# A mixture-of-experts stage with the token chunk as its outer loop and gates read back from DRAM

## The chip, the core and the metric

The kernel runs on one core of a Trainium2 chip. The metric is the device time of the whole program in microseconds. Engines are named as in the profile: PE (TensorE matmul) and PEld (its weight load), DVE (VectorE), ACT (ScalarE), POOL (GpSimd) and SP (SyncE, which here only issues DMAs).

## What is computed

A Mamba-2 block and a mixture-of-experts (MoE) block, each with a layernorm before and after and a residual, on 8 x 256 tokens of 256 channels. The change is in the second block:

```python
router = xf @ gate_w.T                                   # 8 experts
probs = softmax(router); top_p, top_i = top_k(probs, 2)
combine = zeros((n, 8)).at[arange(n)[:, None], top_i].set(top_p)
h = silu(xf @ expert_fc1[e].T) * (xf @ expert_fc2[e].T)  # 176 hidden rows an expert
y = einsum('ne,enc->nc', combine, h @ expert_proj[e].T)  # all 8 experts, then weighted
shared = (silu(xf @ shared_fc1.T) * (xf @ shared_fc2.T)) @ shared_proj.T   # 704 hidden rows
y = y + sigmoid(xf @ shared_gate_w.T) * shared
x = x + layernorm(y)
```

## The kernel before

The first three quarters of the time are the Mamba block, which the change leaves alone but for two tuples of PSUM bank numbers (L196, L197). The MoE block begins at L1205.

**Tiles.** The hidden rows of all eight experts (8 x 176 = 1408, exactly 11 tiles of 128) and of the shared expert (704, five and a half tiles) are laid end to end and padded to FT = 17 tiles. The 2048 tokens are CHUNKS = 4 chunks of UT = 512 columns. One *step* j is one tile f with one chunk c, and there are 68 of them. Every float32 product is made of three passes in the format float32r, high x high, high x low and low x high, so that each weight and activation is first split in two parts: ACT copies the high part, and POOL or DVE subtracts it from the whole to get the low one.

**One step.** PE's `hidden(j)` (L1320) makes fc1 into PSUM bank 4 or 5 and fc2 into bank 6 or 7, six matmuls each. `route_weight` (L1355) makes in bank 0 or 1, by one bf16 matmul of a one-hot matrix `f_hot` with the gates `combT`, the gate of each hidden row. ACT's `silu` (L1479) writes `sl`; DVE's `gated` (L1582) multiplies it by fc2 to `hm`, and `routed` (L1588) by the gate to `hc`. ACT's `high` (L1488) and POOL's `low` (L1734) split `hc` into `h_hi` and `h_lo`. PE's `project` (L1359) makes six matmuls of it into banks 2 and 3, and DVE's `add_up` (L1592) adds these to `outT` in SBUF. PE emits `hidden(j)`, the gate matmul and `project(j - 2)` in this order.

**Order.** The tile is the outer loop: after a head of AHEAD = 3 tiles, taken chunk by chunk before the gates are known (`early`, L1338), tiles 3 to 16 run in a hardware loop (`pair_loop`, L1261), with four chunks each; each tile's weights are loaded (`reload`, L1284) and split (ACT L1461, POOL L1731) as they come up. All four chunks end with the last tile, so the last layernorm (turning the sum back to rows by PE transposes, L1391; statistics, L1696; scaling and residual; the four output DMAs, L1300) stands behind the last step, for all four.

**The way in.** Before the first step the kernel ends the Mamba block's residual and makes the MoE input: `stats`/`scales`/`residual` on DVE (L221 to L251), `stats2`/`scales2` (L1557), the square roots `row_std`, `row_std2` and the scaling `normed` (L1467) on ACT, `turn_normed` (L1305) on PE, `high_x` (L1474) on ACT and `low_x` (L1573) on DVE. Each engine's order is written out by hand.

Of the kernel before, what the change touches and what calls it, by code (L numbers as in the profile page):

```python
# [5 lines left out]
def mamba_moe_sandwich_kernel(nc, x_d, wx_d, wz_d, wo_d, par_d, wdt_d, dtb_d, alog_d,  # L6
# [17 lines left out]
    KH = HID // 128  # L24
# [25 lines left out]
    with outer:  # L50
# [145 lines left out]
        BANK1 = (2, 0, 4, 2)  # L196
        BANKV = (5, 5, 5, 7)  # L197
# [1005 lines left out]


        sb = make_sb(outer)  # L1205
        AHEAD = 3
        END = CHUNKS * FT
        EARLY = CHUNKS * AHEAD
        PSTEPS = [(c, f) for c in range(CHUNKS) for f in range(AHEAD)]
        BUF = (2, 3, 0)  # L1210
        xo = sb("xo", [128, TILES, HID], fp32)
        wf_raw = sb("wf_raw", [128, 2, 768], fp32)
        wf_hi = sb("wf_hi", [128, AHEAD + 1, 768], f32r)
        wf_lo = sb("wf_lo", [128, AHEAD + 1, 768], f32r)
        combT = sb("combT", [CROWS, TOK], bf16)
        f_hot = sb("f_hot", [CROWS, FT * 128], bf16)
# [5 lines left out]
        ident_b = sb("ident_b", [128, 128], bf16)  # L1222
        lgT = sb("lgT", [NLG, TOK], fp32)
# [4 lines left out]
        gts = shared[:, TILES * HID:TILES * (HID + E * E)].rearrange("p (t e o) -> p t e o", t=TILES, e=E)  # L1228
        eqs = sb("eqs", [128, TILES, E, E], fp32)
        rank = sb("rank", [128, TILES, E], fp32)  # L1230
        comb = sb("comb", [128, TILES, ROUTES], fp32)
        comb_r = sb("comb_r", [128, TILES, ROUTES], fp32)
        cparts = sb("cparts", [128, TILES, PARTS, ROUTES], bf16)
        sl = sb("sl", [128, 2, UT], fp32)
        hm = sb("hm", [128, EARLY, UT], fp32)

        hot_raw = hm[0:CROWS, 7:EARLY, :].rearrange("p s t -> p (s t)")[:, 0:FT * 128]
        hc = sb("hc", [128, 2, UT], fp32)
        h_hi = sb("h_hi", [128, CHUNKS, UT], f32r)
        h_lo = sb("h_lo", [128, CHUNKS, UT], f32r)  # L1240
# [6 lines left out]
        s_q, s_e, s_cp = sem("s2_shifted_logits"), sem("s2_exp"), sem("s2_route_parts")  # L1247
        s_ct, s_cc = sem("s2_combT"), sem("s2_combT_copied")
        f1_done, f2_done, g_done, p_done = sem("fc1_done"), sem("fc2_done"), sem("route_weight_done"), sem("moe_proj_done")
        sl_done, hhi_done, wfh_done = sem("fc1_silu_done"), sem("h_hi_done"), sem("moe_w_hi_done")  # L1250
        hm_done, hc_done, fa_done = sem("h_done"), sem("h_scaled"), sem("moe_proj_added")
# [5 lines left out]
        BANK2 = (6, 0, 2, 0)  # L1257
        LBANK = (2, 3, 0, 1)
        BANK4 = (4, 6, 0, 2)

        def pair_loop(eng, body):  # L1261


            body(AHEAD, 1, 1, BUF[AHEAD - 1], False)
            body(AHEAD + 1, 2, 0, 1, False)
            with eng.Fori(1, (FT - AHEAD) // 2 - 1) as i:
                body(2 * i + AHEAD, i + 1, 1, 0, False)
                body(2 * i + AHEAD + 1, i + 2, 0, 1, False)
            body(FT - 2, FT // 2 - 1, 1, 0, True)
            body(FT - 1, FT // 2, 0, 1, True)  # L1270

        SUMB = (2, 6, 4, 2)
        ADDS = CHUNKS - EARLY

        with nc.Block() as block:
            @block.sync
            def _(sp):
                for f in range(2):
                    sp.dma_start(wf_raw[:, f, :], wf_d[f, :, :]).then_inc(s_f[f], 16)
                for dst, src in ((wg_raw[:, :, :], wg_d.rearrange("p (k n) -> p k n", k=KH)),  # L1280
                                 (tie[:, :], tie_d), (hot_raw, f_hot_d)):
                    sp.dma_start(dst, src).then_inc(s_in, 16)

                def reload(f, par):  # L1284
                    sp.wait_ge(wfl_done, f + 1)
                    sp.dma_start(wf_raw[:, par, :], wf_d[f + 2, :, :]).then_inc(s_f[par], 16)

                for f in range(AHEAD):
                    reload(f, f % 2)

                def body(f, filled, par, before, last):
                    if not last:
                        reload(f, par)
                pair_loop(sp, body)
                for i in range(CHUNKS):
                    if i < CHUNKS - 1:
                        sp.wait_ge(s_o4, i + 1)
                    else:
                        sp.wait_ge(s_sc4, TILES)
                    sp.dma_start(out_v[:, quarter(i), :], xo[:, quarter(i), :]).then_inc(s_out, 16)  # L1300
                sp.wait_ge(s_out, 16 * CHUNKS)

            @block.tensor
            def _(pe):
                def turn_normed(i):  # L1305
                    pe.wait_ge(s_n, QT * i + QT)

                    if i == 0:
                        pe.wait_ge(s_rn, 2)
                    elif i == 3:  # L1310
                        pe.wait_ge(s_l2, KH * 2)
                    else:
                        pe.wait_ge(s_x1, QT * (2 if i == 1 else 4))
# [6 lines left out]
                def hidden(j, par, c):  # L1320
                    need(pe, hm_done, j - 1)
                    if isinstance(j, int) and j == 0:
                        pe.wait_ge(s_x1, QT * 3)
                    for which in range(2):
                        n = 0
                        for whl, xhl in ((wf_hi, xnT_hi), (wf_hi, xnT_lo), (wf_lo, xnT_hi)):
                            for k in range(KH):
                                w0 = 256 * k + 128 * which
                                mm = pe.matmul(PS[:, 4 + 2 * which + j_parity(j, c), :], whl[:, par, w0:w0 + 128],  # L1329
# [3 lines left out]
                        mm.then_inc(f2_done if which else f1_done, 1)  # L1333

                def j_parity(j, c):
                    return j % 2 if isinstance(j, int) else c % 2

                def early(p):  # L1338
                    c, f = PSTEPS[p]
                    pe.wait_ge(wfl_done, f + 1)  # L1340
                    pe.wait_ge(s_l2, KH * c + KH)
                    hidden(p, BUF[f], c)

                def logits(i):
                    pe.wait_ge(s_gl, 1)
                    pe.wait_ge(s_l2, KH * 3 if i < 2 else KH * CHUNKS)
# [8 lines left out]
                def route_weight(f, c, bank):  # L1355
                    hot = f_hot[:, 128 * f:128 * f + 128] if isinstance(f, int) else f_hot[:, bass.ds(128 * f, 128)]
                    pe.matmul(PS[:, bank, :], hot, combT[:, UT * c:UT * c + UT], start=True, stop=True).then_inc(g_done, 1)  # L1357

                def project(j, par, c):  # L1359
                    pe.wait_ge(hlo_done, j + 1)  # L1360
                    need(pe, fa_done, j + ADDS)
                    shares(2, par, c, True, True)

                def shares(bank, par, slot, first, last):
                    for m in range(KH):
                        w0 = 512 + 128 * m
# [464 lines left out]
```

## Time and profile before

| | us |
|---|---|
| the three runs | 1510.77, 7722.83, 7724.07 (median 7722.83) |
| the profiled execution, from first to last instruction | 1511.5 |
| of it PE busy | 1416.6 (94%) |
| DVE, ACT, POOL busy | 1192.8, 989.4, 868.5 |
| Mamba block, until its last matmul | to 1138.4 |
| MoE block, its first instruction to the end | 1141.2 to 1511.5 |

Two of the three runs are some 6212 us longer than the third, with which the profiled execution agrees; the profile shows nothing of such a wait. Instructions overlap on PE, so that the duration of a matmul (0.39 us) is about twice the distance between two starts; the distance is what counts. The granted TensorE clock is given as a share of 2.4 GHz: 1.00 is 2.4 GHz and 0.50 is 1.2 GHz.

### The profile page before, as it was taken

To read this page: it belongs to the slowest core of one execution; us is meant where nothing else is said; L and a number is where in the kernel's file an instruction comes from. 1 tells how busy PE (TensorE), PEld (TensorE's weight loads), DVE (VectorE), ACT (ScalarE), POOL (GpSimd) and SP (SyncE) were. 2 spreads that over 40 slices of the span, in tenths; PEclk is the share of its full clock that TensorE was granted. 3 is DMA by queue.
4 is the path that set the end of the run, shared out by engine and by line. 5 is a ranking of instruction groups with operands and counts; after the bars stand their busy time and mean duration, and the time that the engine had idled before them with its cause. 6 is when DMAs were issued, how large, how long until landed. Compare 5 with 4: busy or idle time off the path is not lost. (4 is left out here: it accounts for less than half of the span.)

```text
span 1511.5 us, 25812 instructions
## 1 busy us (share of the span) xinstructions
PE 1416.6 (94%) x7484; PEld 1013.6 (67%) x7484; DVE 1192.8 (79%) x1749; ACT 989.4 (65%) x1450; POOL 868.5 (57%) x758
## 2 busy tenths in 40 slices
PE   4699999999999999999999999999987999999995
PEld 3466667767676776767667677766765667777774
DVE  6799888988997988999898899989757555555556
ACT  4587877878787787877778787877746322333333
POOL 3256676767676666767676676777562143333333
PEclk9799999999999999999999999999988999999998
DMA  4100000010000000000000000000011000000001
GB/s 115 43 13 25 19 18 25 5 33 3 24 18 18 24 3 27 9 24 18 18 25 3 18 18 24 17 18 4 4 57 60 11 11 22 21 21 21 21 0 56
DMA packets 26219, 34.47 MB, mean 23 GB/s; under 512 B 10420, under 2 KB 20276, under 8 KB 26090
## 3 DMA queue, kind: packets, MB, share of 16 engines
q1 hardware_dynamic: 26116, 33.42, 7.3%
q14 instruction: 77, 0.62, 0.1%
q8 instruction: 26, 0.43, 0.1%
HBM read 30.13 MB, written 3.28 MB: 22 GB/s over the span
## 5 line engine op out<-in xcount | busy, mean ns | idle before, releaser
L346 DVE SCALAR_TENSOR_TENSOR acc<-PS,par_a,acc 128x510 f32<-128x510 f32 (+2 forms) x576 | 422.1, 738 | 25.6 <-ACT acc L310 20.0
L1126 POOL TENSOR_TENSOR g_lo<-gy,g_hi 128x512 fp32r<-128x512 f32 x128 | 171.4, 1339 | 215.8 <-ACT g_hi L862 215.7
L1135 POOL TENSOR_TENSOR ssq<-ssq,y 128x256 f32<-128x256 f32 x256 | 262.6, 1026 | 13.2
L1120 POOL TENSOR_TENSOR gy<-y,sz 128x512 f32<-128x512 f32 x128 | 193.4, 1511 | 89.8 <-DVE y L998 57.8
L1736 POOL TENSOR_TENSOR h_lo<-hc,h_hi 128x512 fp32r<-128x512 f32 x68 | 87.6, 1290 | 205.0 <-ACT h_hi L1491 204.9
L985 DVE SCALAR_TENSOR_TENSOR shared<-shared,cbm 128x1024 f32<-128x1024 f32 x96 | 141.4, 1473 | 67.7 <-ACT shared L849 67.6
L310 ACT ACTIVATE acc<-PS,par_a 128x512 f32<-128x512 f32 x192 | 149.3, 777 | 31.2 <-PE PS L293 27.7
L985 DVE SCALAR_TENSOR_TENSOR M<-M,cbm 128x1024 f32<-128x1024 f32 x96 | 150.7, 1569 | 4.9 <-ACT M L849 1.4
L293 PE MATMUL PS<-xnT_hi,wx_hi 128*128 128x512 f32 x384 | 143.3, 454 | 6.5 <-DVE acc L346 5.8
L849 ACT ACTIVATE M<-PS 128x1024 f32<-128x1024 f32 x96 | 98.5, 1026 | 66.8 <-PE PS L687 66.5
L1491 ACT ACTIVATE h_hi<-hc 128x512 fp32r<-128x512 f32 x68 | 43.0, 632 | 151.1 <-DVE hc L1590 151.1
L844 ACT ACTIVATE sz<-PS 128x512 f32<-128x512 f32 x128 | 76.4, 598 | 92.9 <-PE PS L293 89.7
L1582 DVE TENSOR_TENSOR hm<-PS,sl 128x512 f32<-128x512 f32 x68 | 47.0, 691 | 110.0 <-PE PS L1329 100.1
L687 PE MATMUL PS<-R,L 91*128 91x512 bf16 x384 | 117.3, 387 | 16.2 <-ACT shared L849 13.3
L293 PE MATMUL PS<-xnT_hi,wx_lo 128*128 128x512 f32 x384 | 122.5, 401 | 0.0
L730 PE MATMUL PS<-g_hi,wo_hi 128*128 128x512 f32 x256 | 109.1, 426 | 13.6 <-DVE outT L1014 8.0
L293 PE MATMUL PS<-xnT_lo,wx_hi 128*128 128x512 f32 x384 | 121.8, 399 | 0.0
L849 ACT ACTIVATE shared<-PS 128x1024 f32<-128x1024 f32 x96 | 98.3, 1024 | 12.7 <-PE PS L687 12.3
L730 PE MATMUL PS<-g_hi,wo_lo 128*128 128x512 f32 x256 | 103.2, 403 | 0.0
L730 PE MATMUL PS<-g_lo,wo_hi 128*128 128x512 f32 x256 | 102.6, 401 | 0.0
L713 PE MATMUL PS<-M,xdt 128*64 128x256 f32 (+1 forms) x1024 | 97.3, 332 | 0.5 <-issue 0.5
L713 PE MATMUL PS<-shared,xdt 128*64 128x256 f32 (+1 forms) x1024 | 97.3, 332 | 0.1
(198 smaller groups left out, 3194.6 us busy)
## 6 DMA issues: line engine op xcount, KB each, us to landing
wf_raw<-in_wf SPq DMA_DIRECT2D x17, 384.0 KB, 3.1
wraw<-in_wx SPq DMA_DIRECT2D x8, 768.0 KB, 4.5
wraw<-in_wz SPq DMA_DIRECT2D x8, 512.0 KB, 3.4
R<-cs_parts SPq DMA_DIRECT2D x256, 3.0 KB
wraw<-in_wo SPq DMA_DIRECT2D x8, 512.0 KB, 3.4
L<-cs_parts SPq DMA_DIRECT2D x64, 36.0 KB
outT<-in_x SPq DMA_DIRECT2D x4, 512.0 KB, 6.0
shared<-in_x SPq DMA_DIRECT2D x4, 512.0 KB, 3.9
```

The lines of the kernel that those rows point to most:

```text
L293: mm = pe.matmul(PS[:, bank, :], lhs[:, k, c0:c0 + 128], rhs[:, k, UT * q:UT * q + UT], start=(n == 0), stop=(n == 3 * KH - 1))
L310: act.activation(acc[:, k % 3, :], PS[:, XBANK[k], :], ACT.Identity, scale=par_a[:, TAPS * k + TAPS - 1:TAPS * k + TAPS], bias=par_a[:, TA ...
L346: dve.scalar_tensor_tensor(dst[:, :, s:SEQ], src[:, :, 0:SEQ - s], par_a[:, TAPS * k + TAPS - 1 - s:TAPS * k + TAPS - s], dst[:, :, s:SEQ] ...
L687: mm = pe.matmul(PS[:, 2 + s, :], L[:, b, s, 128 * blk:128 * blk + 128], R[:, b, min(blk, 1), s, :, :], start=True, stop=True)
L713: mm = pe.matmul(o, lhs, rhs, start=(c == 0), stop=(c == 1))
L730: mm = pe.matmul(PS[:, bank, :], lhs[:, ct, 128 * m:128 * m + 128], rhs[:, ct, :], start=(ct == 0 and n == 0), stop=(ct == CT - 1 and n == 2))
L849: act.activation(M[par][:, BORDER[n], :, :].rearrange("p h (s i) -> p s h i", s=2), PD.rearrange("p s (h i) -> p s h i", i=64), ACT.Exp).t ...
L985: dve.scalar_tensor_tensor(M[par][:, blk, :, :], M[par][:, blk, :, :], 1.0, cbm[:, 128 * blk:128 * blk + 128].unsqueeze(1).to_broadcast([1 ...
L1120: pool.tensor_tensor(gy[:, half, :, :], y[:, half, :, :], sz[:, 2 * half:2 * half + 2, SEQ * b:SEQ * b + SEQ], ALU.mult).then_inc(gy_done, 1)
L1126: pool.tensor_tensor(g_lo[:, cts, ts], gy[:, half, :, :], g_hi[:, cts, ts].bitcast(fp32), ALU.subtract).then_inc(lo_done, 1)
L1135: pool.tensor_tensor(tok, tok, y2[:, half, cc, :], ALU.add).then_inc(ssq_link, 1)
L1736: pool.tensor_tensor(h_lo[:, c, :], hc[:, c % 2, :], h_hi[:, c, :].bitcast(fp32), ALU.subtract).then_inc(hlo_done, 1)
```

## The change

The stage is rewritten around the token chunk. The 17 tiles' weights stay in SBUF in 11 slots (`SLOTS`): the six shared tiles come first, for all four chunks (24 steps), then the eleven expert tiles for chunk 0, 1, 2, 3 (44 steps), while six of them refill the slots of shared tiles. No hardware loop is left. The projection is summed over a chunk's tiles in PSUM banks 2 and 3 (`ZB`) and read once. The half-filled tile 16 is made by 6 matmuls with fc1 and fc2 side by side, instead of 12. The shared sum is multiplied by its sigmoid afterwards (`gate_shared`); the experts' gates are written to DRAM once, read back with each expert's row repeated over its partitions (`load_gate`, 256 KB a step), and multiplied to the silu on POOL (`gate`). The last layernorm of chunk c runs in steps of chunk c + 1. What was `combT`, `f_hot` and the bf16 parts of the gates is gone.

The diff, cut to its core:

```diff
-        BANK1 = (2, 0, 4, 2)
-        BANKV = (5, 5, 5, 7)
+        BANK1 = (2, 0, 2, 0)
+        BANKV = (5, 5, 5, 5)
...
+        END_S, END_E = 6, 11
+        STEPS = [(c, f) for c in range(CHUNKS) for f in range(END_E, FT)] + \
+                [(c, f) for c in range(CHUNKS) for f in range(END_E)]
+        SLOTS = 11
+        GSLOTS = 4
+        HR = 3
+        NORM_AT = (3, 6, 8)
+        LOGITS_AT = (10, 11)
+        GATES_AT = 12
+        GATES_OUT = 21
+        REFILL = (21, 22, 23, 26, 28, 30)
...  SP
+                def load_tile(n):
+                    if n >= 2:
+                        sp.wait_ge(wfl_done, n - 1)
+                    sp.dma_start(wf_raw[:, n % 2, :], wf_d[TILE_AT[n], :, :]).then_inc(s_f[n % 2], 16)
+                def load_gate(n):
+                    c, f = STEPS[SHARED + n]
+                    if n >= GSLOTS:
+                        sp.wait_ge(sg_done, n - GSLOTS + 1)
+                    for e, p, q in segments(f):
+                        src = gate_rows[e:e + 1, UT * c:UT * c + UT]
+                        sp.dma_start(g_sb[p:q, n % GSLOTS, :], src.to_broadcast([q - p, UT])).then_inc(s_g[n % GSLOTS], 16)
+                sp.wait_ge(s_cc, 1)
+                sp.dma_start(gate_rows[0:E, :].rearrange("e (t p) -> (e t) p", p=128), gT[:, 0, :]).then_inc(s_gd, 16)
+                sp.dma_start(gate_rows[E, :].rearrange("(t p) -> t p", p=128), gT[0:TILES, 1, :]).then_inc(s_gd, 16)
+                sp.wait_ge(s_gd, 32)
+                for n in range(GSLOTS):
+                    load_gate(n)
+                load_shared_gate(0)
...  PE
-                    for which in range(2):
+                    for which in range(1 if f == HALF else 2):
...
-                def route_weight(f, c, bank):
-                    pe.matmul(PS[:, bank, :], hot, combT[:, UT * c:UT * c + UT], start=True, stop=True).then_inc(g_done, 1)
...
+                def project(j):
+                    c, f = STEPS[j]
+                    s, r = SLOT[f], rows_of(f)
+                    pe.wait_ge(hlo_done, j + 1)
+                    if first_of(j):
+                        need(pe, fa_done, c if j < SHARED else CHUNKS + c)
+                    for m in range(KH):
+                        for n, (whl, hhl) in enumerate(((wf_hi, h_hi), (wf_hi, h_lo), (wf_lo, h_hi))):
+                            mm = pe.matmul(PS[:, ZB + m, :], whl[0:r, s, w0:w0 + 128], hhl[0:r, j % HR, :],
+                                           start=(first_of(j) and n == 0), stop=(last_of(j) and n == 2))
+                for j in range(END):
+                    hidden(j)
+                    if j >= 2:
+                        project(j - 2)
+                    if j in NORM_AT:
+                        turn_normed(1 + NORM_AT.index(j))
+                    if j in LOGITS_AT: ...
+                    if j > SHARED + END_E and STEPS[j][1] == 3:
+                        turn_sum(STEPS[j][0] - 1)
+                project(END - 2)
+                project(END - 1)
+                turn_sum(CHUNKS - 1)
...  ACT
+                split(0)
+                row_std2(0)
+                norms(act, 1, TILES - QT, TILES)
+                normed(0)
+                row_std(act, 2)
+                split(1)
+                high_x(0)
+                row_std(act, 3)
+                split(2)
+                for j in range(END):
+                    silu(j)
+                    high(j)
+                    if j == 0: split(3); row_std2(1)
+                    if j == 1: split(4); normed(1); ...
+                    if j == 2: split(5)
+                    if j == 3: row_std2(2); row_std2(3)
+                    if j == NORM_AT[0]: high_x(1)
+                    if j == 5: normed(2)
+                    if j == NORM_AT[1]: high_x(2); normed(3)
...
+                    if j > SHARED + END_E and STEPS[j][1] == 3: row_std4(STEPS[j][0] - 1)
+                    if j > SHARED + END_E and STEPS[j][1] == 4: finish(STEPS[j][0] - 1)
...  DVE
-                    dve.tensor_tensor(hc[:, par, :], PS[:, par, :], hm[:, slot, :], ALU.mult).then_inc(hc_done, 1)
...
+                    if j > SHARED + END_E and STEPS[j][1] == 1: add_experts(STEPS[j][0] - 1)
+                    gated(j)
+                    if j == 0: scales(dve, 3); residual(dve, 3); stats2(1); scales2(1)
+                    if j == 1: stats2(2)
+                    if j == 2: stats2(3)
+                    if j == 4: scales2(2); scales2(3)
+                    if j == NORM_AT[0] + 1: low_x(1)
+                    if j in REFILL: split(SLOTS + REFILL.index(j))
+                    if j >= SHARED and STEPS[j][1] == 8: gate_shared(STEPS[j][0])
+                    if j > SHARED + END_E and STEPS[j][1] == 3: stats4(STEPS[j][0] - 1)
+                    if j > SHARED + END_E and STEPS[j][1] == 4: scales4(STEPS[j][0] - 1)
...  POOL
+                def gate(j):
+                    pool.wait_ge(s_g[n % GSLOTS], 16 * loads)
+                    pool.wait_ge(sl_done, j + 1)
+                    need(pool, hm_done, j - 1)
+                    pool.tensor_tensor(sg[:, j % 2, :], sl[:, j % 2, :], g_sb[:, n % GSLOTS, :], ALU.mult).then_inc(sg_done, 1)
+                for j in range(END):
+                    if j < 3: split(3 + j)
+                    if j >= SHARED: gate(j)
+                    if j > SHARED: low(j - 1)
+                    if j < SHARED: low(j)
+                    if 10 <= j < 10 + SLOTS - END_S: split(END_S + j - 10)
+                    if j > SHARED + END_E and 4 <= STEPS[j][1] < 4 + QT:
+                        pool.tensor_tensor(xo[:, n, :], xo[:, n, :], x1[:, n, :], ALU.add).then_inc(s_o4, 1)
```

(A condition and its calls are put on one line here, and waits that the text does not speak of are left out.)

## Rows read from the trace of the kernel before

**Rows 1.** Busy time by stretch of the MoE block (header, three stretches).
```profile
core 0: us, PE busy (x) PEld busy (x) DVE busy (x) ACT busy (x) POOL busy (x), PEclk, DMA share, GB/s
1150.00:1156.30 6.30, 6.30 (x21) 5.03 (x21) 5.30 (x26) 3.94 (x8) 1.37 (x2) 0.54 0.44 125
...
1223.70:1487.30 263.60, 263.60 (x1066) 189.48 (x1065) 143.69 (x167) 78.71 (x126) 95.56 (x69) 1.00 0.06 17
1487.30:1511.50 24.20, 7.10 (x45) 5.59 (x43) 18.76 (x51) 10.06 (x22) 8.30 (x4) 0.77 0.26 87
```

**Rows 2.** Timeline of one steady step, PE: start, duration, instruction, count.
```profile
1303.71 0.63 PE L1329 MATMUL PS<-xnT_hi,wf_hi 128*128 128x512 f32 x2
...
1306.05 0.63 PE L1329 MATMUL PS<-xnT_hi,wf_lo 128*128 128x512 f32 x2
1306.61 0.38 PE L1357 MATMUL PS<-combT,f_hot 27*128 27x512 bf16 x1
1306.92 0.50 PE L1368 MATMUL PS<-h_hi,wf_hi 128*128 128x512 f32 x1
1307.26 0.39 PE L1368 MATMUL PS<-h_lo,wf_hi 128*128 128x512 f32 x1
```

**Rows 3.** Timeline of the same steady stretch, the other engines.
```profile
1305.31 0.60 ACT L1482 ACTIVATE sl<-PS 128x512 f32<-128x512 f32 x1 [0.98 <-PE PS L1329]
1306.78 0.69 DVE L1582 TENSOR_TENSOR hm<-PS,sl 128x512 f32<-128x512 f32 x1 [1.65 <-PE PS L1329]
1308.31 0.63 ACT L1491 ACTIVATE h_hi<-hc 128x512 fp32r<-128x512 f32 x1 [2.40 <-DVE hc L1590]
1308.62 1.23 DVE L1595 TENSOR_TENSOR outT<-PS,outT 128x1024 f32<-128x1024 f32 x1 [0.42 <-PE PS L1368]
1309.02 1.29 POOL L1736 TENSOR_TENSOR h_lo<-hc,h_hi 128x512 fp32r<-128x512 f32 x1 [3.33 <-ACT h_hi L1491]
```

**Rows 4.** Timeline of the way into the MoE block.
```profile
1141.18 0.82 SPq L1279 DMA_DIRECT2D wf_raw<-in_wf  x2
1143.96 2.07 ACT L1471 ACTIVATE xo<-shared,acc 128x256 f32<-128x256 f32 x4 [0.29 <-DVE acc L1571]
1146.40 0.83 ACT L1461 ACTIVATE wf_hi<-wf_raw 128x768 fp32r<-128x768 f32 x1
1148.59 1.28 DVE L1576 TENSOR_TENSOR xnT_lo<-PS,xnT_hi 128x512 fp32r<-128x512 f32 x2
1149.78 1.39 DVE L1560 BATCH_NORM_STATS2 acc<-shared 128x6 f32<-128x256 f32 x4
1149.96 1.19 PE L1329 MATMUL PS<-xnT_hi,wf_hi 128*128 128x512 f32 x2 [2.78 <-DVE xnT_lo L1576]
1155.53 1.65 DVE L250 SCALAR_TENSOR_TENSOR shared<-PS,acc,shared 128x256 f32<-128x256 f32 x4
1155.76 1.28 ACT L1482 ACT_TABLE_LOAD   x1
1155.82 1.85 POOL L1731 TENSOR_TENSOR wf_lo<-wf_raw,wf_hi 128x768 fp32r<-128x768 f32 x1 [4.93 <-ACT wf_hi L1461]
```

**Rows 5.** DMA issues: tensors, queue, count, size, median us to landing.
```profile
wf_raw<-in_wf SPq DMA_DIRECT2D x17, 384.0 KB, 3.1
```

**Rows 6.** Timeline of the end: last projection, last turn, last scaling.
```profile
1493.11 0.40 PE L1368 MATMUL PS<-h_hi,wf_lo 128*128 128x512 f32 x1
...
1495.11 1.09 PE L1391 MATMUL PS<-ident,outT 128*128 128x128 f32 x8 [0.74 <-DVE outT L1595]
...
1506.50 1.70 ACT L1549 ACTIVATE xo<-xo,acc 128x256 f32<-128x256 f32 x4 [2.94 <-DVE xo L1724]
```

**Rows 7.** Timeline in the Mamba block: one POOL product twice, one DVE product.
```profile
460.62 1.30 POOL L1120 TENSOR_TENSOR gy<-y,sz 128x512 f32<-128x512 f32 x1 [1.33 <-ACT sz L844]
...
469.66 2.28 POOL L1120 TENSOR_TENSOR gy<-y,sz 128x512 f32<-128x512 f32 x1
...
468.92 1.87 DVE L985 SCALAR_TENSOR_TENSOR shared<-shared,cbm 128x1024 f32<-128x1024 f32 x1
```

More of the change, by code:

```diff
@@ L1288, in _ @@
[L1288 to L1300, printed above, removed]
@@ new lines, in _ @@
+                for n in range(END_S, SLOTS + 2):
+                    load_tile(n)
+                sp.wait_ge(s_cc, 1)
[5 more added lines that the diff above has]
+                load_shared_gate(0)
@@ L1525, in _ @@
-                for p in range(7, EARLY - 1):
-                    silu(p, p % 2)
-                for p in range(EARLY):
-                    high(p, p % CHUNKS)
-                    if p == 1:
-                        silu(EARLY - 1, (EARLY - 1) % 2)
-                def body(f, filled, par, before, last):
-                    for c in range(CHUNKS):
-                        j = CHUNKS * f + c
-                        silu(j, c % 2)
-                        high(j, c)
-                        if c == 2 and not (isinstance(f, int) and f == FT - 1):
-                            split(f + 1, filled + par, 1 - par, 1 - par)
@@ L1540, in _, with high, row_std4, finish @@
-                pair_loop(act, body)
-                for i in range(CHUNKS):
+                def high(j):
+                    r = rows_of(STEPS[j][1])
+                    act.wait_ge(hm_done, j + 1)
+                    need(act, p_done, j - HR + 1)
+                    act.activation(h_hi[0:r, j % HR, :], hm[0:r, j % 2, :], ACT.Copy).then_inc(hhi_done, 1)
+                def row_std4(i):
                     act.wait_ge(s_ag4, 2 * i + 2)
                     act.activation(std[0][:, quarter(i)], mv[0][:, quarter(i), 1], ACT.Sqrt, bias=epsc[:, 0:1]).then_inc(s_sd4, 1)
+                def finish(i):
@@ L1682, in body @@
-                def body(f, filled, par, before, last):
-                    for c in range(CHUNKS):
-                        j = CHUNKS * f + c
-                        gated(j, c % 2, c % 2)
-                        dve.wait_ge(hm_done, j + 1)
-                        routed(j, c % 2, c % 2)
-                        if not (isinstance(j, int) and j - 2 < EARLY):
-                            add_up(j - 2, (c - 2) % CHUNKS)
-                        elif PSTEPS[j - 2][1] == AHEAD - 1:
-                            first_sum(PSTEPS[j - 2][0])
@@ L1742, in _ @@
-                split(AHEAD, 1, 1)
-                for p in range(EARLY):
-                    low(p, p % CHUNKS)
-                def body(f, filled, par, before, last):
-                    for c in range(CHUNKS):
-                        low(CHUNKS * f + c, c)
-                        if c == 2 and not (isinstance(f, int) and f == FT - 1):
-                            split(f + 1, 1 - par, 1 - par)
-                pair_loop(pool, body)
-                for i in range(CHUNKS - 1):
-                    pool.wait_ge(s_sc4, QT * i + QT)
-                    pool.tensor_tensor(xo[:, quarter(i), :], xo[:, quarter(i), :], x1[:, quarter(i), :], ALU.add).then_inc(s_o4, 1)
+                for n in range(3):
+                    split(n)
```

644 lines of the change are left out of this document (343 added, 301 removed).

## Prediction

> **What bounds the kernel now.** I read the busy time by stretch first, for where PE is the bound, then the timeline of one steady step, for what PE's time there is made of, then the timelines of the way in and the end, where PE waits. From 1223.7 to 1487.3 PE is busy all the time at the full clock [rows 1]. These are the last 56 of the 68 steps, 263.6 / 56 = 4.707 us each; DVE, ACT and POOL are busy 143.7, 78.7 and 95.6 us of it. So PE's stream is the time, and what leaves it is gained in full as long as the new waits stay inside the slack. At both ends it is otherwise: the first step starts at 1149.96, after a wait of 2.78 us for the low part of the input [rows 4], and runs at a granted clock of 0.54, which is the 1.2 GHz level for most of the stretch [rows 1]; and of the last 24.2 us PE works 7.1.
>
> **PE's stream, term by term.** From 1303.71 to 1306.05 ten matmuls start, one every 0.234 us [rows 2]. Eighteen of them are 4.21 us. A step takes 4.71, so the gate matmul costs 0.50, although it is one of nineteen: it starts 0.33 us after the one before, the next comes 0.31 later and the one after that 0.34 [rows 2], so its neighbours lose time too. It goes from all 68 steps: 68 x 0.50 = 34 us. If what follows it (0.34 against 0.234) were a cost of beginning `project` and stayed, 27 us would go; where `project` ends and `hidden` begins, nothing of the kind is seen, so I take 34. The half tile saves 6 matmuls in 4 chunks, 24 x 0.234 = 5.6 us. Hidden and projection are then 816 - 24 + 408 = 1200 matmuls, logits 24 as before.
>
> I sum the new kernel from its own start, since the way in is reordered.
>
> **The way in.** ACT's queue now begins with `split(0)`, which waits for the weight tile. It is issued at 1141.18 [rows 4] and lands 3.1 us later [rows 5], 1144.3; the split takes 0.83 [rows 4]. Before, the square root and the scaling stood ahead of it, the scaling from 1143.96. So the scaling now runs from about 1145.8 to 1147.9. `row_std(2)` and `split(1)` stand before `high_x(0)`, but `low_x(0)` no longer waits behind `residual(2)` (1.65 us, [rows 4]). I get the first hidden at 1151.2, 1.2 us later than before. It runs at 1.2 GHz again: 12 matmuls cost about 5.1 us instead of 2.8, +2.3.
>
> Then the small work of the second layernorm, which was spread around eleven steps without projection, sits between steps that need the whole chain silu, `gated`, `high`, `low`. I walked the four queues with the durations of [rows 3, 4] (silu 0.60, gated 0.69, high 0.63, low 1.29, split 0.83 on ACT and 1.85 on POOL, scaling 2.07, statistics 1.39, residual 1.65, each change of ACT's table 1.28). ACT changes between square root and silu five times before step 5. PE's waits come out as: `hidden(2)` 0.4 us, for gated(0), behind split(2) and a table; `project(0)` 2.0, for low(0), since POOL has split(3) ahead of it and that waits for ACT; `hidden(3)` 1.1, for gated(1), since silu(1) waits for row_std2(1), which waits for residual and statistics on DVE; `project(1)` 1.9, for low(1), behind split(4); `hidden(6)` 2.2, for the low part of chunk 1, `low_x(1)`, behind the square roots and a table. Together 7.6 us. From `hidden(7)` on, at 1188.4, the queues have caught up.
>
> **Steady shared steps.** 4.21 us, half tile 2.81. DVE has gated and at most one of ranking, splitting, copying a sum (1.23 for 1024 columns, [rows 3]) in one step: hidden behind PE. Gates are transposed and copied in step 21; write, wait, read back is two DMA round trips. At 3.1 us each and six issues of some 0.4 they are back before silu(24), about 11 us later; and `gated(24)` is needed by `hidden(26)` only 7 us after that. Cost nothing; a round trip twice as long would still cost nothing.
>
> **Steady expert steps.** The chain of a step: silu 0.60, POOL's product `gate` (nearest row: POOL's product of two 128x512 tiles, 1.30, [rows 7]), gated 0.69, high 0.63, low 1.29. ACT can't start the next silu before its high, so the loop ACT, POOL, DVE, ACT takes 0.60 + 1.30 + 0.69 + 0.63 and four hand-overs, about 3.6 us against PE's 4.21. low(j) stands behind gate(j + 1) on POOL and ends 3.5 us after fc1 of step j + 1; `project(j)` comes 5.6 us after it. 2.1 us of slack, no cost. POOL is busy 2.6 of 4.2. Loads of 256 KB four steps ahead (17 us) have 3.1 us of landing to hide.
>
> The upper bound for `gate` is 2.28, the same product beside a DVE product of SBUF operands (1.87 [rows 7], where 1024 columns take 1.23 in [rows 3]). The Trainium skill states this ("SBUF — State Buffer", "Who interferes with whom"): a DVE instruction with two SBUF inputs and a GpSimd one that reads SBUF exclude each other. By that rule the moved work is exposed, as POOL now runs twice as often; the trace agrees in the Mamba block. Here `gated` has one input in PSUM, so only the six splits and four `gate_shared` on DVE meet POOL, 1.2 us at most each, inside the 2.1; by the rule as by the row the sum is unchanged.
>
> **Chunk boundaries, three of them.** In step f = 3 PE turns the sum, DVE takes statistics, ACT the square root with two table changes (2.56); in step f = 4 `finish` holds ACT for about 2 us before silu(f5). low(f4) stands on POOL behind gate(f5), which waits for that silu: it ends 1.3 to 1.4 us after PE wants `project(f4)`. 3 x 1.4 = 4.2 us.
>
> **The end.** `project(67)` waits for the last chain: +0.9 us. Behind it stand one add (1.23), one turn, one chunk's statistics, scaling and DMA, about 11.0 us, where before there were 1511.5 - 1493.5 = 18.0, with four chunks' of it [rows 6].
>
> **Sum.** 1151.2 + 1224 x 0.234 (286.4) + 2.3 (clock) + 7.6 (waits of the way in) + transposes: three input turns, three sum turns, the logits, at 1.05 each, and the gates 0.3 (7.6) + 4.2 + 0.9 = 1460.2; + 11.0 = 1471.2. After the waits of the way in the clock may fall once more; I add 0.8 for the chance of it. **1472 us**, against the profiled 1511.5. The median of the runs shown, 7722.83, is that of executions with some 6212 us of which the profile has nothing; the forecast is for an execution like the profiled one and like the lowest run, 1510.77.
>
> **Rivals.**
> 1. *The way in costs more* (17%). For it: the walk has five waits in 30 us, and PE idling there as before the first step is followed by the 1.2 GHz level. If the first 108 matmuls (25 us) run at it for half the way, +12, with waits of +2: 1480 to 1490. Against: the full clock held later in [rows 1].
> 2. *The saving is eaten in every step* (15%). If the order gate(j + 1), low(j) on POOL or the ACT loop makes PE wait 0.3 to 0.5 us in each of 44 expert steps: +13 to +22, 1485 to 1494. Against: 0.6 us to spare in the one, 2.1 in the other.
> 3. *Slower than before* (8%). The ACT-POOL-DVE loop becomes the pace. With `gate` at the blocked 2.28 it is 4.6 us, +0.4 x 44 = 17: still rival 2. From `gate` = 2.8 us on (5.1 a step) it costs 40 us and decides, 1512 or more. The nearest free row is 1.30, and the partner that blocks it is missing in these steps.
> 4. The matmul's cost is not given back since `project` pays it (27 instead of 34) is within the forecast's own range.
>
> **Numbers.** Forecast 60%, its own range 1460 to 1481. Faster by over 2% means under 1481.3; 2% is about what a measurement of this kernel can tell from no change. That is the forecast and a third of rival 1: 0.66. Within 2%: the rest of rival 1, rival 2: 0.26. Slower: 0.08. Range 1458 to 1494: below, 12 us for waits of the way in that don't occur and a DMA that lands sooner; above, rivals 1 and 2.
>
> **What would show it.** Steady steps of 4.21 us with PE without waits; first hidden near 1151; PE's waits before `project(0)`, `project(1)`, `hidden(6)` from POOL's and DVE's low parts; three waits of some 1.4 us in front of `project` of step f = 4, with two table loads each; under 12 us after the last projection. It is wrong if the timeline shows POOL's gate product near 2.3 us, if PE waits in ordinary expert steps, or if the clock is at 1.2 GHz beyond the first two steps.

## The result, and the profile after

| | us |
|---|---|
| kernel before, beside it | 1508.8 and 1510.8 |
| changed kernel, four runs | 1472.35 to 1474.66, median 1473.7 |
| ratio | 0.9761, 95% interval 0.9745 to 0.9776 |
| its profiled execution, first to last instruction | 1472.9 (before: 1511.5) |

It is faster by 2.4%, 1.7 us above the forecast. The 7.72 ms of two listed runs of before came back in none of its later runs, and the ratio leaves them out.

Rows of the page, the changed kernel:

```profile
span 1472.9 us, 25235 instructions
PE 1378.0 (94%) x7378; PEld 1004.1 (68%) x7378; DVE 1092.1 (74%) x1631; ACT 1000.0 (68%) x1465; POOL 916.7 (62%) x806
L1806 POOL TENSOR_TENSOR h_lo<-hm,h_hi 128x512 fp32r<-128x512 f32 x68 | 89.3, 1314 | 48.8 <-ACT h_hi L1523 48.8
L1801 POOL TENSOR_TENSOR sg<-sl,ssq 128x512 f32<-128x512 f32 x44 | 57.0, 1296 | 72.5 <-issue 64.6
```

PE is busy 38.6 us less, with 106 matmuls fewer, and its share of the span is the same: it was and is the bound. DVE is relieved of 101 us, POOL has 48 more. The two POOL products of an expert step take 1.30 and 1.31 us, as the nearest row, the 1.30 of [rows 7], had it.

Busy time by stretch, as in [rows 1]:

```profile
core 0: us, PE busy (x) PEld busy (x) DVE busy (x) ACT busy (x) POOL busy (x), PEclk, DMA share, GB/s
1150.00:1156.30 6.30, 6.18 (x21) 5.01 (x22) 4.16 (x18) 1.88 (x3) 0.79 (x1) 0.76 0.20 62
...
1273.00:1280.00 7.00, 6.33 (x16) 4.99 (x17) 2.73 (x4) 2.23 (x4) 4.23 (x4) 0.55 0.12 47
1280.00:1326.00 46.00, 46.00 (x200) 36.96 (x199) 12.81 (x16) 15.54 (x25) 26.71 (x22) 1.00 0.38 89
```

Ordinary expert steps (third row) keep PE busy at the full clock. The second row is what the prediction did not have: 7 us at a granted clock of 0.55, most of them at the 1.2 GHz level, in the middle of the stage.

Timeline of one ordinary expert step, all engines, as [rows 2, 3]:

```profile
1312.70 0.39 PE L1408 MATMUL PS<-h_hi,wf_hi 128*128 128x512 f32 x1
1312.93 0.40 PE L1408 MATMUL PS<-h_lo,wf_hi 128*128 128x512 f32 x1
...
1313.46 1.29 POOL L1806 TENSOR_TENSOR h_lo<-hm,h_hi 128x512 fp32r<-128x512 f32 x1
1313.64 0.69 DVE L1640 TENSOR_TENSOR hm<-PS,sg 128x512 f32<-128x512 f32 x1 [3.50 <-POOL sg L1801]
1314.36 0.63 ACT L1523 ACTIVATE h_hi<-hm 128x512 fp32r<-128x512 f32 x1 [2.27 <-DVE hm L1640]
1315.69 0.60 ACT L1511 ACTIVATE sl<-PS 128x512 f32<-128x512 f32 x1 [0.69 <-PE PS L1388]
1316.42 1.28 POOL L1801 TENSOR_TENSOR sg<-sl,ssq 128x512 f32<-128x512 f32 x1 [1.66 <-issue]
1316.89 0.39 PE L1408 MATMUL PS<-h_hi,wf_hi 128*128 128x512 f32 x1
```

`project` begins at 1312.70 and again at 1316.89, a step of 4.19 us against 4.71. Its second matmul starts 0.23 us after the first, where it was 0.34 in [rows 2]. `h_lo` ends at 1314.75, 2.1 us before `project` wants it, and ACT waits 0.69 us for PE before the silu: both slacks are there.

All of PE's waits of the stage, the table of waits of the changed kernel from 1150 us on (engine, line, what it waited for: us in total, times, longest):

```profile
PE PS L1408 <- POOL h_lo L1806: 6.1, 6, 1.5
PE PS L1388 <- DVE hm L1640: 4.1, 3, 2.6
PE PS L1388 <- DVE xnT_lo L1621: 2.8, 2, 1.5
PE PS L1445 <- DVE outT L1665: 1.3, 1, 1.3
```

**A measure free of the Mamba block.** The last Mamba matmul (L730) starts at a time that varies between profiles, from 1133.9 to 1139.5 us, though the Mamba block's code is the same but for the bank numbers: 1133.9 to 1139.0 in the three profiles with the bank numbers of before, 1134.4 to 1139.5 in the eleven with the new ones. In these two:

```profile
1138.21 0.40 PE L730 MATMUL PS<-g_hi,wo_lo 128*128 128x512 f32 x1
```

```profile
1135.73 0.40 PE L730 MATMUL PS<-g_hi,wo_lo 128*128 128x512 f32 x1
```

The first is before, the second the changed kernel. From this start to the end of the span is called the *tail stretch* below: 373.3 us before, 337.2 after. So the change took 36.1 us out of what it touches, and 2.5 of the 38.6 us between the two spans are the Mamba block's. Of the 36.1, the steps from the first hidden to the last projection gave 30.8 (343.5 before, 312.7 after) and what stands behind them 8.0 (18.0 and 10.0); the way in took back 2.6 (11.8 and 14.4). The 8.0 is read from the two traces; no experiment took the ending by itself. The one kernel that was profiled twice has tail stretches of 327.7 and 327.9 us, where its runs spread over 6 us; so small effects are read from it. With one profile for each of the others, a difference of less than some 1 us is not shown by it: the first matmuls of the stage alone run 6 to 14 at a time at the 1.2 GHz level in profiles of the same way in, which is up to 1.5 us.

### The profile page after: what moved, and what is told of

It is laid out like the page before. It is cut to its first block and busy times, and to the rows that moved or that the text cites. A ratio compares the mean times of both kernels' runs of the same rounds, so it can differ in the third digit from the quotient of the medians.

```text
span 1472.9 us, 25235 instructions
## 1 busy us (share of the span) xinstructions
PE 1378.0 (94%) x7378; PEld 1004.1 (68%) x7378; DVE 1092.1 (74%) x1631; ACT 1000.0 (68%) x1465; POOL 916.7 (62%) x806
## 5 line engine op out<-in xcount | busy, mean ns | idle before, releaser
L1135 POOL TENSOR_TENSOR ssq<-ssq,y 128x256 f32<-128x256 f32 x256 | 265.8, 1038 | 13.2
L1523 ACT ACTIVATE h_hi<-hm 128x512 fp32r<-128x512 f32 x68 | 43.0, 632 | 143.0 <-DVE hm L1640 139.1
L730 PE MATMUL PS<-g_hi,wo_hi 128*128 128x512 f32 x256 | 108.6, 424 | 13.5 <-DVE outT L1014 8.2
L1806 POOL TENSOR_TENSOR h_lo<-hm,h_hi 128x512 fp32r<-128x512 f32 x68 | 89.3, 1314 | 48.8 <-ACT h_hi L1523 48.8
L1640 DVE TENSOR_TENSOR hm<-PS,sg 128x512 f32<-128x512 f32 x44 | 30.4, 691 | 117.7 <-POOL sg L1801 117.7
L730 PE MATMUL PS<-g_hi,wo_lo 128*128 128x512 f32 x256 | 102.9, 402 | 0.0
L730 PE MATMUL PS<-g_lo,wo_hi 128*128 128x512 f32 x256 | 102.4, 400 | 0.0
L1801 POOL TENSOR_TENSOR sg<-sl,ssq 128x512 f32<-128x512 f32 x44 | 57.0, 1296 | 72.5 <-issue 64.6
```

Source lines behind the costliest of these rows:

```text
L730: mm = pe.matmul(PS[:, bank, :], lhs[:, ct, 128 * m:128 * m + 128], rhs[:, ct, :], start=(ct == 0 and n == 0), stop=(ct == CT - 1 and n == 2))
L1135: pool.tensor_tensor(tok, tok, y2[:, half, cc, :], ALU.add).then_inc(ssq_link, 1)
L1806: pool.tensor_tensor(h_lo[0:r, j % HR, :], hm[0:r, j % 2, :], h_hi[0:r, j % HR, :].bitcast(fp32), ALU.subtract).then_inc(hlo_done, 1)
```

## The experiments

Eleven further kernels ran, one of them twice. One profile of each run gives the tail stretch (us); ratios are to the kernel before on the same chip.

| | median us | ratio (95%) | tail stretch |
|---|---|---|---|
| before | 1509.5 to 1509.8 | | 373.3 |
| no gate matmul (before) | 1482.1 | 0.982 (0.980 to 0.985) | 345.0 |
| no add (before) | 1508.7 | 0.999 (0.998 to 1.000) | 372.2 |
| the changed kernel | 1473.7 | 0.976 (0.975 to 0.978) | 337.2 |
| gate product twice | 1510.6 | 1.000 (0.999 to 1.002) | 371.8 |
| tile 13 first | 1470.3 | 0.974 (0.972 to 0.975) | 331.7 |
| full half tile | 1476.6 | 0.977 (0.975 to 0.980) | 337.2 |
| spread finish | 1470.4 | 0.974 (0.972 to 0.976) | 333.7 |
| way in reordered | 1472.8 | 0.975 (0.973 to 0.976) | 335.5 |
| all three | 1465.4 | 0.971 (0.969 to 0.973) | 327.7 |
| all three, again | 1468.7 | 0.972 (0.970 to 0.974) | 327.9 |
| all three, full half tile | 1469.3 | 0.973 (0.972 to 0.975) | 332.1 |
| tile 13 first and spread | 1468.6 | 0.972 (0.970 to 0.974) | 328.5 |
| the same, full half tile | 1467.4 | 0.973 (0.971 to 0.975) | 331.0 |

**The gate matmul alone.** Its edit, in the kernel before; the gates are then not applied, so `hc` is made from whatever its PSUM bank holds:

```diff
-                    pe.matmul(PS[:, bank, :], hot, combT[:, UT * c:UT * c + UT], start=True, stop=True).then_inc(g_done, 1)
+                    return
...
-                    dve.wait_ge(g_done, j + 1)
```

> The kernel before without its gate matmul (nor the wait for it); the DVE product reads the same PSUM bank, which now holds stale values, so the experts are not weighted by their gates. If the matmul and what it takes from its neighbours cost 0.50 us in each of 68 steps, the time falls by 34 us to about 1476, and a steady step is 4.21 us. If the slow first matmul of the projection is a cost of beginning the projection, it stays: 0.40 a step, 27 us, 1483. If another engine's wait took its place, less than 20 us.

Timeline of PE in the kernel without it:

```profile
1304.49 0.63 PE L1329 MATMUL PS<-xnT_hi,wf_lo 128*128 128x512 f32 x2
1304.96 0.39 PE L1368 MATMUL PS<-h_hi,wf_hi 128*128 128x512 f32 x1
1305.18 0.40 PE L1368 MATMUL PS<-h_lo,wf_hi 128*128 128x512 f32 x1
...
1306.34 0.63 PE L1329 MATMUL PS<-xnT_hi,wf_hi 128*128 128x512 f32 x2
```

The 0.34 us behind the gate matmul in [rows 2] are gone (1304.96, 1305.18), so they were no cost of beginning `project`: rival 4 fell, and an undisturbed step is 4.18 us, 0.52 less. Yet the whole gave 28.3 us of tail stretch, not 34. Of four steps in this kernel three last 4.18, 4.18 and about 4.26, and the fourth 4.40, with a gap of 0.2 us ahead of `hidden` that the trace puts down to nothing; over the last 56 steps the mean is 4.25, 0.45 less than before instead of 0.50, which loses 2.5 us. And in the first twelve steps PE waits three times for the old chain's low part, 3.9 us from start to start. 34 - 2.5 - 3.9 = 27.6, near the 28.3. The median (1482.1) lies where the rival that was wrong about the cause had put it.

**The add alone.** In the kernel before, DVE's `add_up` cut to 8 of 512 columns (the sum is wrong elsewhere). It stands for "summed in PSUM".

```diff
-                    dve.tensor_tensor(o, PS[:, 2:2 + KH, :], o, ALU.add).then_inc(fa_done, 1)
+                    dve.tensor_tensor(o[:, :, 0:8], PS[:, 2:2 + KH, 0:8], o[:, :, 0:8], ALU.add).then_inc(fa_done, 1)
```

> The kernel before with the sum of each projection into SBUF cut from 512 to 8 columns a half (1.23 us to some 0.1 on DVE, 56 times; the output is wrong by it). If PE's stream is the bound and the sum in PSUM gained nothing by itself, the time stays within 1.5 us of before. If DVE's add held PE back (through fa_done), up to 0.3 us a step, 17 us shorter.

58 us less of DVE and 0.1% of the time. DVE was not the bound, so the projection's sum in PSUM brings nothing by itself; it brings room for the work that now lies between the steps.

**The gate product twice.** In the changed kernel, POOL makes each gate product first into a scratch and then again:

```diff
+                    pool.tensor_tensor(scratch[:, UT * (1 + j % 2):UT * (2 + j % 2)], sl[:, j % 2, :], g_sb[:, n % GSLOTS, :], ALU.mult)
                     pool.tensor_tensor(sg[:, j % 2, :], sl[:, j % 2, :], g_sb[:, n % GSLOTS, :], ALU.mult).then_inc(sg_done, 1)
```

> The changed kernel with POOL's gate product done twice in each expert step (the first result goes to an unused place). The loop silu, gate, gated, high then has 1.28 us more. In the trace of the changed kernel the loop without waits is 3.4 us; with the second product 4.7, above PE's 4.21 a step: 44 x 0.47 = 20 us longer, about 1493, and the loop is the pace. If slack were larger (gate off the loop), about 1474. If POOL's two operations a step were the bound it would take 3.85 us a step and also cost nothing.

Timeline of one such step, one turn of the loop, and the row of its waits from 1280 us on:

```profile
1370.58 0.58 ACT L1511 ACTIVATE sl<-PS 128x512 f32<-128x512 f32 x1
1371.29 1.38 POOL L1801 TENSOR_TENSOR scratch<-sl,ssq 128x512 f32<-128x512 f32 x1 [0.86 <-issue]
...
1372.63 1.28 POOL L1802 TENSOR_TENSOR sg<-sl,ssq 128x512 f32<-128x512 f32 x1
1374.05 0.69 DVE L1640 TENSOR_TENSOR hm<-PS,sg 128x512 f32<-128x512 f32 x1 [2.53 <-POOL sg L1802]
1374.78 0.63 ACT L1523 ACTIVATE h_hi<-hm 128x512 fp32r<-128x512 f32 x1 [3.62 <-DVE hm L1640]
1375.31 0.58 ACT L1511 ACTIVATE sl<-PS 128x512 f32<-128x512 f32 x1
```

```profile
PE PS L1408 <- POOL h_lo L1807: 23.8, 39, 2.9
```

The mechanism is the one foretold: the silu waits for its own ACT's `high`, and the loop sets the pace, 4.64 us in most steps (4.73 in this one). So with one product it is 3.4 us, where the prediction said 3.6. But the price was 34.6 us, not 20. PE's starts in both kernels split it: 23 ordinary steps 0.45 longer each, 10.5 us; each of the three chunk boundaries (four steps) 4.5 to 4.6 us longer, 14 us; the first eight expert steps 6 us, where ACT's split of a weight tile (0.83) stands in the loop in three of them, and DVE's makes POOL's first product 1.52 us instead of 1.29; the last two projections 4 us, where PE waits 2.89 us for the last chain and the clock falls. So a loop without slack takes in neither table load nor split nor `finish`; each goes straight into PE's time.

**The late tile.** The trace of the changed kernel shows PE idle 2.63 us before `hidden(26)`, and the reason on ACT and SP:

```profile
1255.96 0.33 SPq L1330 DMA_DIRECT2D gate_rows<-gT  x1
1256.33 0.43 SPq L1331 DMA_DIRECT2D gate_rows<-gT  x1
1257.84 3.45 SPq L1314 DMA_DIRECT2D ssq<-gate_rows  x6
1261.33 0.43 SPq L1319 DMA_DIRECT2D scratch<-gate_rows  x1
1261.81 10.22 SPq L1305 DMA_DIRECT2D wf_raw<-in_wf  x3
...
1269.83 0.85 ACT L1489 ACTIVATE wf_hi<-wf_raw 128x768 fp32r<-128x768 f32 x1 [6.07 <-DMA wf_raw<-in_wf]
1270.70 0.60 ACT L1511 ACTIVATE sl<-PS 128x512 f32<-128x512 f32 x1
...
1273.67 1.22 PE L1388 MATMUL PS<-xnT_hi,wf_hi 128*128 128x512 f32 x2 [2.63 <-DVE hm L1640]
1274.69 1.05 PE L1388 MATMUL PS<-xnT_lo,wf_hi 128*128 128x512 f32 x2
```

Its DMA view of 1254 to 1276 us (size and median us to landing):

```profile
wf_raw<-in_wf SPq DMA_DIRECT2D x3, 384.0 KB, 8.0
```

`load_tile(13)` stands on SP behind the gates' round trip and seven issues (the recorded text below counts five), is issued at 1261.81, and takes 8.0 us to land among the gate rows, where [rows 5] had 3.1. ACT meets its `split(13)` in step 23 and idles 6.07 us; `silu(24)` is behind it, then gate, `gated`, and `hidden(26)` waits for that. After the gap, two matmuls take 1.05 where they took 0.63: the 1.2 GHz level, for 12 matmuls, 2.5 us more. From `project(23)` to `hidden(27)` PE takes 11.2 us, where the edited kernel below takes 5.9: 5.3 us in all. The edit issues the tile ahead of the gate rows:

```diff
                 sp.wait_ge(s_gd, 32)
+                load_tile(SLOTS + 2)
                 for n in range(GSLOTS):
                     load_gate(n)
```

> The changed kernel with one DMA moved: weight tile number 13 is issued ahead of the gate rows instead of behind five loads of them. In the trace of the changed kernel that tile lands 8 us after its issue, ACT waits 6.1 us for it in front of silu(24), and PE waits 2.6 us for gated(24) and then runs twelve matmuls at 1.2 GHz (+2.5). If the tile's place is the cause, 5 us shorter than the changed kernel, about 1468.5. If the read-back of the gates is late itself, moving it behind the tile keeps the wait or makes it longer: 1473 to 1476.

```profile
1257.60 0.34 SPq L1305 DMA_DIRECT2D wf_raw<-in_wf  x1
1257.98 3.60 SPq L1314 DMA_DIRECT2D ssq<-gate_rows  x6
...
1263.45 0.83 ACT L1490 ACTIVATE wf_hi<-wf_raw 128x768 fp32r<-128x768 f32 x1
1264.31 0.60 ACT L1512 ACTIVATE sl<-PS 128x512 f32<-128x512 f32 x1
```

In this timeline of the edited kernel the tile is issued 4.2 us earlier and lands in 3.1 us, ACT's split no longer waits, PE has neither gap nor slow clock there, and the tail stretch is 5.5 us shorter. The first gate row, now behind the tile, still lands in time: POOL's product follows `silu(24)` without a wait. Here the cause is shown, not argued.

**The boundaries.** `finish` was spread over four steps instead of one, and POOL's additions moved one step later:

```diff
-                    if j > SHARED + END_E and STEPS[j][1] == 4:
-                        finish(STEPS[j][0] - 1)
+                    if j > SHARED + END_E and 4 <= STEPS[j][1] < 4 + QT:
+                        finish(STEPS[j][0] - 1, [STEPS[j][1] - 4])
```

> The changed kernel with the four scalings of a chunk's last layernorm on ACT put one each in steps f = 4 to 7, instead of all four in f = 4, and POOL's additions one step later. If they hold up silu of f = 5 and with it the low part of f = 4, the three waits of 1.0 us in front of the projection go: 3 us shorter, about 1470.5. If the two table loads of f = 3 are what makes PE wait, they stay: 1473.5.

In the changed kernel `project` of step f = 4 reads, as at the two other boundaries:

```profile
1344.07 0.50 PE L1408 MATMUL PS<-h_hi,wf_hi 128*128 128x512 f32 x1 [0.85 <-POOL h_lo L1806]
```

With the edit these three waits are gone and the tail stretch is 3.5 us shorter, so 1.1 to 1.2 us for each boundary. The two table loads of step f = 3 are still there (1.28 us each), so they were not the cause.

**The way in.** `stats2(1)` and its square root are taken before the first step:

```diff
-                row_std(act, 3)
                 split(2)
+                row_std2(1)
+                row_std(act, 3)
```

> The changed kernel with the statistics and the square root of chunk 1 ahead of the first silu, and split(2) ahead of that square root: two table loads (2.56 us) and the wait for the statistics leave ACT's queue before silu(1). PE's waits before the first, second and fourth projection steps (0.9, 1.5, 0.6, 1.5 us) should fall to about half; DVE reaches the variance of chunk 3 about 1.8 us later, which may delay silu(0) by 1 us. Expected 2 us shorter, 1471.5. If POOL's order (the split ahead of the low part) sets these waits alone, no change.

Its timeline of PE:

```profile
1159.16 0.62 PE L1388 MATMUL PS<-xnT_hi,wf_lo 128*128 128x512 f32 x2
1163.30 1.22 PE L1388 MATMUL PS<-xnT_hi,wf_hi 128*128 128x512 f32 x2 [3.52 <-DVE hm L1640]
```

Two changes of table are saved, and the five waits of the way in go, 6.6 us from start to start. In their place stands one of 3.52 us before `hidden(2)` (3.7 from start to start), since the first silu now stands behind both square roots, and after it the clock is at 1.2 GHz for 12 matmuls once more, 2.5 us. That leaves 0.4. The other 1.3 us of the 1.7 in the table come from the late tile of step 26, after which only 6 matmuls are slow here instead of 12. So the reordering itself bought nearly nothing: it gathered five waits into one that costs the clock. And the 1.3 us are no merit of it either: why fewer matmuls were slow at step 26 this time is open.

**All three together** (the best kernel of this study):

> The changed kernel with all three edits: tile 13 first, the scalings spread, the square root of chunk 1 early. If the three are independent pieces of PE's path the gains add: 5 + 3 + 2 = 10 us, about 1463.5. If one wait is covered by another, less: 1466 to 1468.

337.2 - 327.7 = 9.5 us, where the three parts give 5.5 + 3.5 + 0.4 = 9.4. A second run of the same kernel:

> The version with all three repairs once more, as the base of the three runs beside it. Its stretch from the last Mamba matmul to the end was 327.7 us; 327 to 329 expected again, median about 1465.

Almost the same stretch, though the medians of the two are 1465.4 and 1468.7: the second's five runs are 1463.3, 1464.1, 1468.7, 1469.4 and 1469.5. That is in keeping with the 5.6 us by which the Mamba block's end varies between profiles; what makes it vary is open. The two profiles came to the same stretch by different ways. In the first the stage begins 0.7 us later and with seven slow pairs of matmuls, then has waits of 2.19 us before `hidden(2)` and 1.50 before `project(1)` at the full clock; in the second three to four pairs are slow, then one wait of 3.42 us before `hidden(2)` is followed by 12 matmuls at the 1.2 GHz level. So the agreement of 9.5 with 9.4 is in part luck on the way in; the two larger parts, whose waits are gone from the trace, are not touched by it.

**The half tile.** Made by 12 matmuls again, in three kernels:

```diff
-        HALF = FT - 1
+        HALF = -1
```

> The changed kernel with the half-filled tile 16 made as every other tile (12 matmuls for fc1 and fc2, 128 rows, the lower ones zero). If PE's matmul count alone counts, 24 x 0.234 = 5.6 us longer than the changed kernel, 1479. In its trace the matmuls next to those of 64 rows start about 0.1 us late, four times in each of the four steps; if that is a cost of changing the rows it falls away: net 5.6 - 1.6 = 4 us, 1477.5. If the steps after it wait for other engines anyway, less than 2 us.

> All three repairs, but the half-filled tile made by 12 matmuls. In the changed kernel without the repairs this edit moved the stretch after the Mamba block by nothing (337.2 and 337.2 us). Theory A: the half tile is worth its 24 matmuls less what its neighbours lose (24 x 0.234 - 4 x 0.4 = 4.0 us), and there the waits for the input's low part and for the late weight tile took it back; with the repairs those are gone, so this kernel is 4.0 us slower than the one with the half tile: 331.7, median 1469. Theory B: the shorter step buys nothing anywhere, since what PE saves it waits for next: same stretch, 327.7 to 328.5.

In the changed kernel it makes no difference (337.2 and 337.2); with the three repairs it is worth 332.1 - 327.9 = 4.2 us. Theory A holds: in the changed kernel two waits ate it. The one for the low part of chunk 1 (1.34 us, 1.5 from start to start) is missing with the full tile. So the half tile brings PE to `hidden(26)` only 2.5 us earlier, counted from the last Mamba matmul (135.3 for 137.8). There it meets the late tile. ACT's split of it comes only 1.4 us earlier (134.1 for 135.5), since the gates' round trip, which SP issues ahead of the tile, begins when PE has turned the gates in step 21, and there, ahead of the fourth half tile, PE is only 1.2 us earlier. So PE waits 1.1 us longer (2.63 us against 1.53), and then loses the clock as well (2.5), where the kernel with the full tile has a second wait of 0.76 us (1.0 from start to start) at the full clock. Timeline of ACT in the kernel with the full tile, its stall:

```profile
1274.99 0.85 ACT L1489 ACTIVATE wf_hi<-wf_raw 128x768 fp32r<-128x768 f32 x1 [6.05 <-DMA wf_raw<-in_wf]
```

> Weight tile 13 ahead of the gate rows and the last scaling spread, the way in as in the changed kernel. Alone they were worth 5.5 and 3.5 us of the stretch after the Mamba block, so 328.2 us if the two are independent (337.2 - 9.0). With the way in reordered as well it was 327.7. Theory A (each wait of the way in that is removed comes back as another, and the clock falls once more): 328 to 329, median about 1466. Theory B (the reordering of the way in is worth its 1.7 us in full): 329.4 here.

> As the one before, with the half-filled tile made by 12 matmuls. Here the wait for the input's low part stands right behind the first shared tiles, so of the four half-tile steps one is swallowed: Theory A: 4.0 - 1.3 = 2.7 us slower than the one before, about 331, median about 1469. Theory B: same as the one before.

Without the way-in edit the two other repairs give 328.5 (foretold 328.2): by that, reordering the way in is worth 0.6 to 0.8 us, too little for these profiles to show. This profile also began with seven slow pairs of matmuls instead of three, 1.5 us more, and `hidden(2)` then had no wait (0.9 us in the changed kernel): part of the clock's loss was taken out of the wait behind it. The full half tile costs 2.5 us there (foretold 2.7), because the shorter one is followed by the wait for the low part of chunk 1 (1.3 us) that the longer one hides. The four medians of this comparison, 1467.4 to 1469.3, don't resolve any of it.

## Why the prediction was right or wrong, point by point

The total came out near, but one step failed: the gates' way through DRAM, put at "Cost nothing", cost 5.5 us. And the total flatters the forecast. Of the span, 39.5 us were to go; from the last Mamba matmul to the end 36.1 went, and the other 2.5 came from an earlier end of the Mamba block in this profile.

The prediction placed the first hidden at 1151.2, the last projection's end at 1460.2 and the end at 1471.2, and added 0.8. Measured: 1150.1, 1462.9 and 1472.9. So the first hidden is 1.1 us early, the steps take 3.7 us more (312.7 for 309.0), and the end 1.0 less. One of the prediction's own signs of being wrong occurred: the clock is at 1.2 GHz beyond the first two steps, at `hidden(26)`.

- **PE's stream is the time**: right. **Gate matmul 0.50, all of it given back**: right and slightly low; steps are 4.19 to 4.21, 0.50 to 0.52 less.
- **Half tile 5.6 us**: the 24 matmuls are right, but where the number of weight rows changes from 128 to 64 and back the neighbours lose some 0.1 us each, 0.4 a step, 1.6 in all. The term should have been 4.0; 4.2 was measured with the late tile and the wait for chunk 1's low part away, 2.5 with that wait there, 0 with both there.
- **First hidden 1.2 us later**: 2.6 us, relative to the Mamba block. The mechanism was right: ACT's queue begins with `split(0)`, which waits for the load (landed 6.0 us after the last Mamba matmul). What was not seen is the small DVE instruction ahead of the scaling:

```profile
1142.67 1.80 POOL L1791 TENSOR_TENSOR wf_lo<-wf_raw,wf_hi 128x768 fp32r<-128x768 f32 x1 [6.30 <-ACT wf_hi L1489]
...
1143.02 1.47 DVE L1616 SCALAR_TENSOR_TENSOR acc<-acc 128x4 f32<-128x4 f32 x1
```

  It ends when POOL's split ends; before, with POOL idle, the same instruction took 0.17. That is 1.3 us. So it is in all eleven profiles of the changed kernel and those made from it (1.46 or 1.47), and in none of the three of before and those made from before (0.16 or 0.17). The reciprocal just ahead of it has one input and took 0.18 beside the same split. It is the exclusion that the Trainium skill states ("SBUF — State Buffer", "Who interferes with whom"); the trace agrees. The prediction applied it to large products only.
- **Clock on the way in +2.3**: 1.3 in this profile, where only 6 matmuls, not 12, are at 1.2 GHz. Other profiles with the same way in have up to 14 (gate product twice; tile 13 first and spread), so that the term itself varies by 1.5 us; what decides it is open.
- **Five waits of the way in**: all five are at the places named, 0.90, 1.49, 0.59, 1.47 and 1.34 us against 0.4, 2.0, 1.1, 1.9 and 2.2; 5.8 in total against 7.6.
- **"Cost nothing" for the gates' way through DRAM**: this step failed. It is the largest error, 5.5 us by experiment. The round trip itself was indeed early enough; the prediction asked only when the gates are back, and priced neither the loads queued on SP *behind* the round trip (tile 13 issued 4.2 us later) nor that a tile's landing grows from 3.1 to 8.0 us among the gate rows. What stood in place of nothing was a wait of 2.63 us at `hidden(26)` and 12 matmuls at the 1.2 GHz level behind it. It would have been found by asking for each `load_tile` what SP holds before it.
- **Steady expert steps**: right. Slack 2.1 foretold and measured; the loop 3.4 for 3.6; `gate` 1.30 for 1.30, between 1.28 and 1.45 in 44 instances. No wait in an ordinary step.
- **Boundaries 1.4 each**: waits of 0.85, 1.1 with what the starts around them lose; 3.5 us for three by experiment against 4.2. Two table loads each, as foretold.
- **The end**: the wait is one projection earlier than foretold, before `project(66)` (0.54), and with slow first matmuls the last twelve lose 1.0 (foretold 0.9). Behind them come 10.0 us, for 11.0; the prediction had not priced its parts one by one, so which was too long can't be told:

```profile
1462.46 0.40 PE L1408 MATMUL PS<-h_hi,wf_lo 128*128 128x512 f32 x1
1462.89 1.23 DVE L1665 TENSOR_TENSOR outT<-PS,outT 128x1024 f32<-128x1024 f32 x1 [3.78 <-PE PS L1408]
...
1468.57 1.70 ACT L1537 ACTIVATE xo<-xo,acc 128x256 f32<-128x256 f32 x4 [1.09 <-DVE xo L1775]
```

  Between this row of the scaling and that of [rows 6] lies the gain of one chunk's ending instead of four: 6.1 us from the last projection to it, against 13.4.
- **Rivals.** 1 and 2 did not occur. 3 was placed too far away: it was to reach the time of before at a gate product of 2.8 us; with 2.6 the measured kernel is already there (ratio 1.000), because the boundaries lose their cover too. Nothing came near it in the changed kernel. 4 fell by experiment.

In the steps, 5.5 us of a missed stall and 1.6 at the half tile stand against 1.8 (waits) and 1.0 (clock) on the way in and 0.7 to 0.9 at the boundaries; that is some 3.5 of the 3.7 us. The first hidden was early only since the Mamba block ended 2.5 us earlier in this profile. That the total is within 2 us is luck: its terms erred by 5.5 one way, and several smaller ones the other.

## What to carry to other kernels

When loads pass through one queue, walk the queue and not only the data: each new round trip on it delays every load behind it, and new transfers lengthen the landings beside them. A saving on the bounding engine in front of a wait whose end it does not move can be worth nothing until the wait is gone, and may cost the clock as well: 4.0 us of the half tile came to 0 here. And a loop that has no slack is dearer than its excess per step, since all that it used to hide comes out with it.

## What was not expected of the hardware

- A DVE instruction on 128x4 values took 1.47 us instead of 0.17 while POOL worked on a 128x768 subtraction; its size says nothing of what POOL costs it.
- A matmul that follows another of a different number of rows, or a wait, is slower to be followed: 0.33 us to the next start instead of 0.234. The bf16 gate matmul of before had the same on both sides [rows 2], which is how one matmul in nineteen could cost 0.50.
- A gap of 2.6 us in PE's work brought the granted clock to the 1.2 GHz level for the next 12 matmuls, and one of 2.5 us with the finish spread likewise; another of 2.5 us in the kernel with the way in reordered did it for 6. One of 2.2 us on the way in with all three edits and one of 1.5 us at step 26 with the full half tile did not, and with the gate product twice three gaps of 2.7 us at the chunk boundaries did it once. So the length of the gap alone does not tell what the clock does.
- A 384 KB load took 8.0 us to land behind and beside the gate rows' reads, 3.1 when it was issued ahead of them, and 3.0 elsewhere in the same kernel (median).
